# First layer norm in sets of samples, with GpSimd as a second normalizer and the convolution's first loads and products inside it

## The reference, cut to what matters

```python
x = x + jnp.tanh(g_xattn[0]) * _L0_xattn_ref(ctx_2048, ctx_2048, _layernorm(x, axis=-1), L0_xattn_ssm_kernel, L0_xattn_D, 8)
x = x + jnp.tanh(g_ffn[0]) * _L0_ffn_ref(_layernorm(x, axis=-1), ...)
x = x + jnp.tanh(g_xattn[1]) * _L1_xattn_ref(_layernorm(x, axis=-1), ctx_2048, ctx_2048)
x = x + jnp.tanh(g_ffn[1]) * _L1_ffn_ref(_layernorm(x, axis=-1), ...)

def _layernorm(x, axis=-1, eps=1e-05):
    m = jnp.mean(x, axis=axis, keepdims=True)
    v = jnp.var(x, axis=axis, keepdims=True)
    return (x - m) / jnp.sqrt(v + eps)

# _L0_xattn_ref(k, v, q, ...): 32 heads of 8 columns, k = v = ctx
kv = jnp.einsum('bhil,bhjl->bijhl', k_, v_)      # products of column pairs
y = causal long convolution of kv with ssm_kernel, through the FFT
out = y + kv * D[None, None, None, :, None]
out = jnp.einsum('bijhl,bhil->bjhl', out, q_)    # q_ is the normed x
```

## Time and profile before

| | us |
|---|---|
| three runs | 1789.28, 1790.46 (median), 1792.06 |
| profiled execution, device time | 1788.26 |
| its span, first to last instruction | 1786.5 |
| first norm, start to last copy into `QT` | 0 to 59.0 |
| first matmul of the convolution | 65.94 |
| last matmul of the convolution | some 401 |

### The profile page before, as it was taken

One profiled execution on the slowest core, in us unless ns is written; L12 is line 12 of the kernel. 1 busy time (PEld: TensorE's weight loads), 2 busy tenths in 40 slices (PEclk: granted clock), 3 DMA queues, 4 the chain that ended last, 5 costly groups with the idle time before them and its releaser, 6 DMA issues. The chain is left out here.

```text
span 1786.5 us, 24803 instructions
## 1 busy us (share of the span) xinstructions
PE 1601.9 (90%) x6978; PEld 888.1 (50%) x6978; DVE 951.1 (53%) x1725; ACT 726.8 (41%) x1403; POOL 949.3 (53%) x961
## 2 busy tenths in 40 slices
PE   4799999997595299999999999868999999999997
PEld 3577777765352044444444443554444444444443
DVE  6488888887536367777777774571111111111111
ACT  7423223325327357777777777531111111111111
POOL 0588888875107457888888888102333333333332
PEclk9999999998697589999999999958999999999999
DMA  6343444427457865666666661832334333443333
GB/s 190 103 144 129 130 137 154 147 94 190 95 165 254 251 138 145 159 156 156 156 155 153 156 157 37 312 112 44 65 69 71 71 63 68 71 71 65 66 71 47
DMA packets 110375, 224.00 MB, mean 125 GB/s; under 512 B 12256, under 2 KB 12256, under 8 KB 109408
## 3 DMA queue, kind: packets, MB, share of 16 engines
q1 hardware_dynamic: 94400, 185.88, 36.8%
q0 software_dynamic: 15904, 37.23, 11.8%
HBM read 146.71 MB, written 75.84 MB: 125 GB/s over the span
## 5 line engine op out<-in xcount | busy, mean ns | idle before, releaser
L1617 DVE TENSOR_REDUCE low<-pA 128x2 f32<-128x1024 f32 x256 | 307.4, 1223 | 144.2 <-PE pA L1350 133.4
L443 PE MATMUL y<-kv,toep 128*128 128x288 f32 x1280 | 328.0, 413 | 15.1 <-POOL kv L374 8.0
L1549 ACT ACTIVATE pt<-pB 128x512 f32<-128x512 f32 x512 | 287.1, 593 | 124.7 <-PE pB L1368 118.9
L1856 POOL DMA_INDIRECT out_rows<-XN,slots x71 | 112.7, 1588 | 356.7 <-DVE XN L1845 356.7
L443 PEld LDWEIGHTS y<-kv,toep 128*128 128x128 f32 x1280 | 239.2, 191 | 103.8 <-DVEq L63 34.1
L1788 PE MATMUL pH<-WF,XN 128*128 x568 | 258.2, 598 | 1.0 <-DVE XN L1836 0.9
L1803 PE MATMUL pY<-WP,XN 128*128 x568 | 255.6, 593 | 0.8 <-ACT XN L1829 0.8
L1368 PE MATMUL pB<-qs,ks 98*128 98x512 f32 x512 | 226.7, 446 | 2.9 <-ACT pt L1549 2.4
L1350 PE MATMUL pA<-ks,qs 96*128 96x512 f32 x512 | 189.2, 415 | 37.0 <-DMA qs<-q_low 35.3
L1368 PEld LDWEIGHTS pB<-qs,ks 98*128 98x128 f32 x512 | 95.8, 189 | 191.4 <-ACT pt L1549 149.1
L1836 DVE COPY XN<-p9T 128x512 f32<-128x512 f32 x71 | 49.1, 692 | 260.5 <-PE p9T L1780 260.5
(11 more groups left out here) (252 smaller groups left out, 2040.8 us busy)
## 6 DMA issues: line engine op xcount, KB each, us to landing
ks<-ctx_high SPq DMA_DIRECT2D x64, 256.0 KB, 4.7
qs<-q_high SPq DMA_DIRECT2D x64, 256.0 KB, 6.3
kc<-in_ctx_conv SPq DMA_DIRECT2D x32, 384.0 KB, 5.1
XN<-in_x SPq DMA_DIRECT2D x16, 512.0 KB, 4.2
toep<-kernel_and_skip SPq DMA_DIRECT2D x32, 256.0 KB, 3.5
ct<-in_ctx SPq DMA_DIRECT2D x16, 512.0 KB, 6.5
ctx_high<-kh SPq DMA_DIRECT2D x16, 512.0 KB, 4.5
ctx_low<-kl SPq DMA_DIRECT2D x16, 512.0 KB, 5.2
```

The source lines that it names most:

```text
L443: m = pe.matmul(y[half].rearrange("p (l n) c -> p l n c", l=CB)[:, l, :, 0:PAIRS], toep[u][:, (l - s) * P:(l - s + 1) * P], kv[u][:, half, ...
L1549: act.activation(pt[s][:, h, :], bank(u, n), ACT.Exp, scale=SCALE1).then_inc(s_exp, 1)
L1617: dve.tensor_reduce(ap(low[u % 2], t % CB * NH + t // CB, [[NH, 2], [1, 1]]), pA[n % 2], op=ALU.max, axis=AX.X, negate=True).then_inc(s_re ...
L1856: pool.indirect_dma_start(out=out["out"], out_offset=bass.IndirectOffsetOnAxis(ap=slots[:, j:j + 1], axis=0), in_=ys[j % 2], in_offset=Non ...
```

## The change

- **Sets.** The samples go in six sets: `SETS = [(0, 1), (1, 2), (2, 4), (4, 8), (8, 12), (12, 16)]`. Statistics, one root on ACT and one row of the six small DVE steps serve a whole set: 6 roots for 16, and 36 small steps for 96. The tiles `stats`, `mv`, `std`, `work`, `rstd`, `shift` now hold all 32 row blocks. The code is written out, without a hardware loop.
- **DVE's order.** Statistics of set g+1 are interleaved with the steps of set g, one `bn_stats` ahead of each step, and the first of them waits until the whole set g+1 has landed. All `bn_aggr` of the set follow behind.
- **Two normalizers.** ACT writes the first row block of a sample, POOL the second (`tensor_scalar`). `qt` and `pq` have four buffers.
- **Loads.** SP issues all sixteen loads of `x` without a wait between them. Behind them come `kc` of head 0 and the gates, then `KP`, `toep` of head 0, `kc` of head 1, `ct` of sample 0 and `toep` of head 1, all in the first block.
- **Pair products.** POOL makes both halves of head 0's `kv` in the first block, behind its norms of samples 4 to 7 and 8 to 11. It also adds `skip` to `kp`, at its start.
- **tanh.** ACT's `tanh` of the gates moves behind the first `qc` copy of the second block.
- `toep`, `kc`, `kv` and `ct` live in a scope that holds both blocks.

The diff, cut to its core:

```diff
+        def pairs_of(pool, h, half):
+            m = CB * B8
+            u, n0 = h % 2, half * m
+            pool.wait_ge(s_kc[u], h // 2 * 16 + 16)
+            pool.tensor_tensor(ap(kv[u], n0 * PAIRS, [[PAIRS, m], [HD0, D4], [1, HD0]]),
+                               ap(kc[u], n0 * CYC, [[CYC, m], [0, D4], [1, HD0]]),
+                               ap(kc[u], n0 * CYC, [[CYC, m], [1, D4], [1, HD0]]), ALU.mult).then_inc(s_kv, 1)
...
...
+            SETS = [(0, 1), (1, 2), (2, 4), (4, 8), (8, 12), (12, 16)]
+            STEPS1 = 6
+            qt = [sb(st, f"qt{i}", [P, TH, C]) for i in range(4)]
+            pq = [pb(st, f"pq{i}", [P, CB, T]) for i in range(4)]
...
             def _(sp):
-                def load(b, u):
-                    sp.dma_start(ap(XN, TH * b * ROW, [[ROW, TH], [1, C]]), a["x"][b].rearrange("(th p) c -> p th c", p=P)).then_inc(s_x[u], 16)
-                load(0, 0)
-                load(1, 1)
+                def load(g):
+                    for b in range(*SETS[g]):
+                        sp.dma_start(ap(XN, TH * b * ROW, [[ROW, TH], [1, C]]), a["x"][b].rearrange("(th p) c -> p th c", p=P)).then_inc(s_x[g], 16)
+                for g in range(2):
+                    load(g)
                 sp.dma_start(kp, a["kern_pad"]).then_inc(s_kp, 16)
                 sp.dma_start(skip, a["skip"].rearrange("(h o) -> h o", o=1)).then_inc(s_kp, 16)
+                for g in range(2, len(SETS)):
+                    load(g)
+                load_pairs(sp, 0)
                 sp.dma_start(gates_raw, a["g"].partition_broadcast(P)).then_inc(s_g, 16)
-                with sp.Fori(1, B // 2) as i:
-                    for u in range(2):
-                        sp.wait_ge(s_x[u], 16 * i)
-                        load(2 * i + u, u)
                 sp.wait_ge(s_skip, 1)
                 sp.dma_start(KP, kp).then_inc(s_kps, 16)
                 sp.wait_ge(s_kps, 16)
+                load_taps(sp, 0)
+                load_pairs(sp, 1)
+                load_ctx(sp, 0)
+                load_taps(sp, 1)
...
             def _(dve):
+                for g in range(len(SETS)):
+                    lo, hi = (TH * b for b in SETS[g + 1]) if g + 1 < len(SETS) else (0, 0)
+                    for k in range(max(STEPS1, hi - lo)):
+                        if lo + k < hi:
+                            look(g + 1, lo + k)
+                        if k < STEPS1:
+                            root(g, k)
+                    for n in range(lo, hi):
+                        close(n)
...
             def _(pool):
+                def norm(g, b):
+                    n = TH * b + 1
+                    pool.wait_ge(s_rt, STEPS1 * g + STEPS1)
+                    after(s_tr, pool, b - 3)
+                    pool.tensor_scalar(qt[b % 4][:, 1], ap(XN, n * ROW, [[1, C]]), rstd[:, n:n + 1], shift[:, n:n + 1],
+                                       ALU.mult, ALU.add).then_inc(s_qp, 1)
...
+                for g, (lo, hi) in enumerate(SETS):
+                    for b in range(lo, hi):
+                        norm(g, b)
+                    if g >= len(SETS) - 3 and g < len(SETS) - 1:
+                        pairs_of(pool, 0, g - (len(SETS) - 3))
...
             def _(act):
-                act.wait_ge(s_g, 16)
-                act.activation(gates, gates_raw, ACT.Tanh).then_inc(s_gates, 1)
+                root(0)
+                for g, (lo, hi) in enumerate(SETS):
+                    for b in range(lo, hi):
+                        norm(g, b)
+                        if b > 1:
+                            keep(b - 2)
+                    if g + 1 < len(SETS):
+                        root(g + 1)
+                keep(B - 2)
+                keep(B - 1)
...
                 copies(0)
+                act.wait_ge(s_g, 16)
+                act.activation(gates, gates_raw, ACT.Tanh).then_inc(s_gates, 1)
```

More of the change, by code:

```diff
@@ new lines, in _build, with load_pairs @@
+        toep = [sb(pre, f"toep{i}", [P, C]) for i in range(2)]
+        kc = [sb(pre, f"kc{i}", [P, HALF * CB * B8, CYC]) for i in range(2)]
+        kv = [sb(pre, f"kv{i}", [P, HALF, CB, B8 * PAIRS]) for i in range(2)]
+        ct = sb(pre, "ct", [P, TH, C])
+        s_kc = [sem(f"s_kc{i}", pre) for i in range(2)]
+        s_tp = [sem(f"s_tp{i}", pre) for i in range(2)]
+        s_kv = sem("s_kv", pre)
+        s_c = sem("s_c_2", pre)
+        s_g = sem("s_g", pre)
+        D4 = NDG - 1
+        def load_pairs(sp, h):
+            sp.dma_start(kc[h % 2].rearrange("p n c -> p (n c)"), a["ctx_conv"][h]).then_inc(s_kc[h % 2], 16)
@@ new lines, in _ @@
+                for n in range(TH):
+                    look(0, n)
+                for n in range(TH):
+                    close(n)
[7 more added lines that the diff above has]
+                    for n in range(lo, hi):
+                        close(n)
@@ L391, in low @@
                     pool.tensor_tensor(kl[:, th].bitcast(F32R), ct[:, th], kh[:, th], ALU.subtract).then_inc(s_kl, 1)
-                for half in range(HALF):
-                    pairs_of(0, half)
                 for h in range(H0):
```

218 lines of the change are left out of this document (77 added, 141 removed).

## The result

| | us |
|---|---|
| changed kernel, median of 7 runs | 1779.76 (1775.59 to 1783.47) |
| before, median of 7 runs | 1789.91 (1788.38 to 1792.10) |
| ratio | 0.9940, 95% interval 0.9928 to 0.9952 |
| forecast | 1777.7, range 1774.5 to 1784.5 |
| norm ends (last copy into `QT`), before and after | 59.03, 54.58 |

The kernel got faster by 10.2 us, where 12.8 were forecast. The profiled execution of the changed kernel took 1781.29, 1.5 over its median, while that of before (1788.26) lies 1.7 under the median of the seven; so the two spans (1786.5 and 1779.6) show only 6.9.

What follows compares the result with a forecast made beforehand. The first 66 us were taken as bound by short handovers in the norm and 6.9 us without heavy work before the convolution. Norm 5.6, hand-over 6.2 and PE's clock 1.0 sum to 12.8 us: 1790.5 to 1777.7, range 1774.5 to 1784.5.

Steps and rivals of the forecast that it cites:

- the tail: Norm's last four samples: PE's pace of 1.76 us a sample, then the last copy of 1.1; norm ends at 53.4.
- the hand-over: Norm's end to the convolution's first matmul: 0.75 us, first matmul at 54.15; 6.2 of the 11.8 us saved.
- the clock's 1.0: Convolution's start: PE idling about 2 us instead of 8 gives back between nothing and 2 us, taken as 1.0.
- in the norm no engine is full: Old norm: a ring of short handovers between ACT and DVE, 2.83 us a sample.
- The start: Norm's start: first root at 7.7 us, 2.3 earlier; `tanh` moved to the convolution and hidden, 1.5 without cover.
- The loads: Norm's queued loads flow at 390 GB/s, 1.34 us a sample: sample 3 at about 8.5, sample 7 at 14.0.
- The chain of sets: Norm's new bound: root, DVE steps, norms of each set; ACT stands 3.5 us per set; sample 12's norm at 44.1.
- the fourth rival: Entry into the convolution's block: PE's instruction issue may show up to 2 us, time 1779.7; chance 0.10.
- The third rival: Norm: POOL's products hold DVE's two-input root steps, 3.8 us for once in each root, time 1781.5; chance 0.08.
- The conversion: Behind the convolution's first matmul: each microsecond by which it comes earlier should come off the end; 11.8 us there.
- The signs of being wrong: First matmul past 57 us, DVE's root steps waiting with POOL as neighbour, or a convolution longer than 335 us.

## Why the prediction was right, and by how much it was off

The sign, the range and the mechanism of the change held; the gain was forecast 2.6 us too large. The terms that were off, at the first matmul: the late data +1.7 us, the tail -0.6, the hand-over +0.5, together the 1.7 by which it came late; with the clock's 1.0, which didn't come, they make up the 2.6.

One reading of the kernel before was wrong. It says that in the norm no engine is full and puts a sample at 2.4 us of ACT against 2.83 taken. That leaves out the root (0.2 from its start to the next instruction) and part of the copy; ACT needs some 2.7, and was the full engine (length, ACT busy, granted clock, DMA share, GB/s):

```profile
20.00:54.00 34.00, 32.59 (x62) 1.00 0.38 120
```

The forecast doesn't rest on it, since it counts the new norm from its parts. But it is why a second normalizer was worth so much, and why sets without it end the norm at 65.73, later than before.

In the order of the prediction's steps:

- **The start** came half a microsecond late: ACT's first root ended at 8.18 (7.7 forecast), 0.4 of it because the first sample was there at 5.00, not 4.58. It cost nothing, since DVE then waited for samples 3 and 7. `tanh` is hidden behind the first matmuls: ACT waits 2.51 us for PE ahead of its first `ym`.
- **The loads** held in rate, not in the first samples: 345 GB/s from 5 to 10 us and 388 behind; from sample 3 (10.27) to sample 7 (15.69) it is 1.355 us a sample, against 1.34. But sample 3 came at 10.27, not at 8.5: the first samples took 1.76 each, and the taps lie among them. This is the term that was mis-sized: DVE waited 1.98 us for sample 7, and the norm of sample 2 came at 19.80 instead of 18.1. How much of it is the taps and how much the start of the queue no run tells apart; in the run with the hand-over undone, whose loads start the same way, sample 7 was there at 15.05. `kc` landed at 27.1 to 27.6 in the four runs where POOL waited for it with all loads queued (26 forecast), so the rate held to the end.
- **The chain of sets** held to 0.1 us from there: 7.2, 10.6 and 8.3 us between the first norms of sets 2, 3, 4 and 5, as worked out (7.2, 10.6, 8.2). The run that took the steps out of the statistics, and the two that took queued loads or POOL's norms away, show each link.
- **The tail** was 8.7 us, not 9.3 (its parts as listed make 9.1). The forecast has PE's pace of 1.76 a sample bound it; in the trace ACT bounds it at 1.66, and PE, with eight transposes in 1.1 us, waits 0.5 to 0.6 for it each time. So the size was near, the engine was another.
- **The hand-over** took 1.24 us from the last copy to the first matmul where 0.75 was put; the copy on ACT came after 0.59, as before, and PE 0.65 behind it. This is a part of the fourth rival, at half a microsecond. The same way took 1.11 in the old norm with the hand-over.
- **PE's clock** was put at 1.0 us and brought nothing that the traces can tell: the first 40 matmul records took 11.84 and 12.88 us in the two traces of before, 11.65 and 12.84 in the two of the changed kernel. The step failed in its ground, that an idle of about 2 us instead of 8 gives back part of the pace. PE idled 3.0 us, but a gap of 2.2 gave nothing back either (11.59 and 11.65); one of 1.05, filled with extra transposes before, did (9.96). That the slow first matmuls are the clock was right, as that run shows.
- **The third rival** didn't occur, for the reason given: POOL was idle in both root stretches. It was the right danger, though: in the old norm the same products cost 3.4 us, and put on the changed kernel's steps 2.7, against 3.8 forecast. With the loads held back, and with POOL's norms taken away, it came by itself.
- **The conversion** of an earlier first matmul into time: 10.1 us there and 10.2 in the medians. That they agree to 0.1 is luck. The interval of the ratio leaves 8.6 to 12.9 us, the two traces of the changed kernel have 7.0 and 1.7 us left at the last pY, and in the other runs 5.8 us became 2.9, and 5.9 became 7.4. "Nothing there looks back at the norm" holds to the end of the convolution (334.5 us from first to last matmul, 334.7 before); behind it the rise of PE's clock in the attention took 0 to 5 us, and the prediction has no term for that.
- **The signs of being wrong**: the limit of 335 us for the convolution was too tight. The second traces have 335.5, and 335.6 for the kernel before.

## What to carry to other kernels

Batching small steps moves the wait from each item to each change of batch, so look there at what stands between the first and last step of the short chain: interleaving that had room to cost little with two instructions a sample cost 6 us with sets of eight. Before a second engine gets work in parallel, list which short instructions of VectorE read two SBUF tensors at that time; a GpSimd product over them multiplies a 0.15 us step by ten. Check the list again after every edit: two experiments here, one that held the loads back and one that took GpSimd's norms away, made the same collision unasked. Before calling a stage a ring of short waits, take the busy share of each engine inside it. And don't read a gain of a few microseconds at the end off one trace: find the place where two traces of different kernels part, and see whether it has to do with the edit. Here a rise of TensorE's clock 500 us later took up to 5 us, more than several of the edits were worth.

## What the runs showed of the hardware

- A DVE step of 0.16 us with two SBUF inputs took 1.55 and 1.81 us beside POOL's 1.89 us product in the old norm, and 1.29, 1.73, 1.54 and 1.49 in four places of edits of the changed one, and ended with it; one with a single input took 0.39 instead of 0.17 beside a product of 0.45.
- POOL's `tensor_scalar` of 128x512 in float32, with scale and shift from columns, takes 0.77 us; ACT's for the same work takes 0.71 from start to start.
- Loads of 512 KB queued in one queue landed 1.355 us apart from sample 3 to sample 7 (388 GB/s from 10 to 15 us); with two in flight the transfer engines were busy for three quarters of the time and moved 228 GB/s (10 to 40 us of the run with loads two ahead).
- PE's clock read 0.50 for 3.4 us at the convolution's start after 3.0 us of idling, and for 6.5 us, from 0.8 us ahead of the first matmul, in a second trace of the same kernel; after 1.05 and 1.08 us of idling it stayed at 1.00. In the last set, with transposes in 1.1 of 1.66 us, it read 1.00 throughout in one trace and 0.50 from 48 to 51 us in the other.
- The clock's column read 1.00 over the whole old norm, where eight transposes took 1.97 us; at a granted 0.50 they took 1.95, and late in the changed kernel's norm 1.1.
- In the attention the clock stood at 0.50 until 22, 29 to 30 or 33 to 35 us behind the first pA, the same in both traces of before and in both of the changed kernel, and the stretch took 0 to 1.2, 2.2 to 3.5 and 3.9 to 5.3 us longer.
